# 128-row products around attention, and operand loads in two column parts, in a one-core window-attention block

## The reference

```python
hp = jnp.pad(layer_norm(x, ln1_g, ln1_b), ...)      # 16 x 16 -> 28 x 28, windows of 14 x 14
q, k, v = split_heads(windows(hp) @ qkv_w + qkv_b)  # 12 heads of 16
attn = (q * scale) @ k.T + bias_h(q, rel_h) + bias_w(q, rel_w)
o = softmax(attn) @ v
x2 = x + unwindow(o @ proj_w + proj_b)[:, :16, :16]
h2 = layer_norm(x2, ln2_g, ln2_b)
out = x2 + gelu(h2 @ mlp_w1 + mlp_b1, approximate=False) @ mlp_w2 + mlp_b2
```

## Time and profile before

| | |
|---|---|
| time of the runs | 338.98 us median of 3 (336.39 to 343.41) |
| the profiled execution | 338.49 us, span 336.6 us |
| busy | PE 294.4 us (87%), DVE 165.6 (49%), ACT 129.2 (38%), POOL 84.4 (25%) |
| one product of L933 | over 128 rows 654 ns, over 64 rows 642 ns (mean, 24 each) |
| granted TensorE clock | 0.912 on average |
| chain that ended last | PE 60%, DMA 21% (of it `qop<-bias` 16%), SP's queue 8%, DVE 6% |

### The profile page before, as it was taken

The page is one execution under the profiler, slowest core; times in us unless marked ns, Lnnn a source line. Parts: engine busy times, 40 slices in busy tenths (PEclk is TensorE's granted clock), DMA queues, the critical chain, the costliest instruction groups (busy, mean ns, idle before and its releaser), DMA issues.

```text
span 336.6 us, 5235 instructions
## 1 busy us (share of the span) xinstructions
PE 294.4 (87%) x1980; PEld 201.8 (60%) x1980; DVE 165.6 (49%) x435; ACT 129.2 (38%) x245; POOL 84.4 (25%) x131
## 2 busy tenths in 40 slices
PE   0799979999889778878888878699898999999996
PEld 0433376557466556656566556448766657868696
DVE  4953384126567567646675677246489211111011
ACT  1144654223546456535553555453001444140400
POOL 3294631003001133303341433470046600000000
PEclk9999998999959999979997999858755699999999
DMA  6660042994005679765864585830000000101011
GB/s 185 172 159 0 2 81 50 177 179 83 1 2 100 121 127 167 126 127 99 173 139 103 105 170 147 214 90 13 14 0 1 0 2 0 47 2 47 0 49 47
DMA packets 19409, 27.94 MB, mean 83 GB/s; under 512 B 6052, under 2 KB 16196, under 8 KB 17560
## 3 DMA queue, kind: packets, MB, share of 16 engines
q1 hardware_dynamic: 16840, 24.95, 34.9%
q0 software_dynamic: 2016, 2.46, 3.8%
q10 hardware_dynamic: 528, 0.20, 0.4%
HBM read 5.81 MB, written 1.57 MB: 22 GB/s over the span
## 4 chain that ended last, share of the span: by engine, by line
PE 60%; DMA 21%; SPq 8%; DVE 6%; issue 2%; ACT 1%; ACTq 0%; DVEq 0%
DMA qop<-bias 16%; PE ps L1229 12%; PE ps L1244 9%; PE ps L933 7%; PE ps L988 6%; PE ps L968 5%; PE ps L1193 3%; PE ps L1022 3%; PE ps L1087 2%; PE ps L1061 2%; SPq L300 2%; DMA qop<-shift_rest 2%; SPq L301 2%; PE ps L917 2%; PE ps L1134 2%
## 5 line engine op out<-in xcount | busy, mean ns | idle before, releaser
L756 DVE TENSOR_REDUCE nmax<-ps 98x2 f32<-98x392 f32 x96 | 53.4, 566 | 41.3 <-PE ps L1022 39.9
L1022 PE MATMUL ps<-kop,qop 126*98 126x196 f32 x192 | 39.2, 291 | 10.8 <-DMA qop<-bias 8.3
L565 ACT ACTIVATE pm<-ps 98x784 f32<-98x784 f32 x48 | 39.4, 830 | 18.5 <-PE ps L1061 18.4
L1022 PEld LDWEIGHTS ps<-kop,qop 126*98 126x98 f32 x192 | 25.7, 176 | 22.3 <-DMA qop<-bias 12.3
L1244 PE MATMUL ps<-w2t,gl 128*128 128x192 f32 x192 | 32.0, 328 | 0.0
L1061 PE MATMUL ps<-qop,kop 128*98 128x196 f32 x192 | 29.0, 278 | 3.3 <-DMA qop<-shift 2.5
L1244 PEld LDWEIGHTS ps<-w2t,gl 128*128 128x128 f32 x192 | 31.1, 190 | 0.7 <-issue 0.7
L761 DVE TENSOR_REDUCE nmax<-ps 120x1 f32<-120x316 f32 x48 | 23.1, 485 | 15.9 <-PE ps L1028 14.6
L633 ACT ACTIVATE gl<-ps,b 128x512 f32<-128x512 f32 x24 | 16.4, 688 | 35.2 <-PE ps L1229 35.1
L437 POOL DMA_DIRECT2D den<-osb x11 | 7.1, 645 | 80.8 <-ACT osb L582 80.8
L1061 PEld LDWEIGHTS ps<-qop,kop 128*98 128x98 f32 x192 | 23.9, 186 | 5.2 <-DMA qop<-shift 2.6
(11 more groups left out here) (129 smaller groups left out, 457.9 us busy)
## 6 DMA issues: line engine op xcount, KB each, us to landing
qop<-bias SPq DMA_DIRECT2D x8, 448.0 KB
kop<-hl SPq DMA_DIRECT2D x12, 280.5 KB
qop<-hl SPq DMA_DIRECT2D x12, 256.0 KB
kop<-hl SPq DMA_DIRECT2D x12, 140.2 KB
bias<-in_x SPq DMA_DIRECT2D x4, 384.0 KB, 4.6
qop<-hl SPq DMA_DIRECT2D x12, 128.0 KB
xres<-in_x SPq DMA_DIRECT2D x2, 768.0 KB, 7.4
out<-xn SPq DMA_DIRECT2D x8, 192.0 KB, 2.0
```

What stands on the lines that cost most here:

```text
L565: a.activation(pm[0:HALF, gi], ps[0:HALF, b0:b0 + 2, 0:2 * WIN], ACT.Exp).then_inc(s["exp_done"], 1)
L756: v_.tensor_reduce(nmax[0:HALF, h % 2, 2 * n:2 * n + 2], ps[0:HALF, bank, 0:2 * WIN].rearrange("p (t k) -> p t k", t=2), AX.X, ALU.max, ne ...
L1022: o = mm(ps[0:HALF, bank, WIN * t:WIN * (t + 1)], q[0:R_MAX, WIN * n + HALF * t:WIN * n + HALF * (t + 1)], kk[0:R_MAX, WIN * n:WIN * (n + ...
```

## The change

It has two parts, which are independent in the code.

**Operand loads in two column parts.** `load_operands(h, part)` loads the columns 0 to 1568 of `qop` and `kop` (part 0) or the rest of both (part 1), with the same DMAs on fewer columns. Part 0 waits for `st_done` of 6 (h - 3) + 4, the last reader of the main columns (`weights(h-3, 3)`), part 1 for all six. `load_low_biases` does the same on POOL. The rest parts have semaphores of their own, for which `score_piece(h, 8)` waits.

**Products over 128 rows.** The tiles `ht1`, `wq1`, `wqp[1]`, `on1`, `wp1` and `w11l` have 128 rows. POOL clears rows 64 to 127 of `ht1`, `wq1`, `wp1` and `on1` by four memsets; the products that read these tiles run over 128 rows. The last product of `hidden` takes `w11l` and `h2s` over all 128 rows, so a product of two low parts is added to the result. `on1` moves from the address of `split` to that of `pm`.

```diff
@@ load_operands @@
-            def load_operands(h):
+            def load_operands(h, part):
                 (tq, rq), (tk, rk) = place(h)
-                q, k, sl = qop[h % RING].bitcast(F32), kop[h % RING].bitcast(F32), op_in[h % RING]
+                c0, c1, c2 = ((0, MAIN, MAIN), (MAIN, T, KCOLS))[part]
+                q, k, sl = qop[h % RING].bitcast(F32), kop[h % RING].bitcast(F32), (op_in, rest_in)[part][h % RING]
                 if h >= RING:
-                    sp.wait_ge(s["st_done"], 6 * (h - RING + 1))
+                    sp.wait_ge(s["st_done"], 6 * (h - RING) + (4, 6)[part])
...
-                src = hl[tq][rq:P:A8, :, 0:T]
-                sp.dma_start(q[0:2 * KD], src).then_inc(sl, 16)
-                sp.dma_start(q[2 * KD:R_BIAS], src[:, 0]).then_inc(sl, 16)
+                src = hl[tq][rq:P:A8, :, c0:c1]
+                sp.dma_start(q[0:2 * KD, c0:c1], src).then_inc(sl, 16)
+                sp.dma_start(q[2 * KD:R_BIAS, c0:c1], src[:, 0]).then_inc(sl, 16)
...
                 if h and h + 2 < HEADS:
-                    load_operands(h + 2)
+                    for part in range(2):
+                        load_operands(h + 2, part)
@@ POOL @@
+            for n, a_ in enumerate((ht1, wq1)):
+                g.memset(a_[C - P:P], 0.0).then_inc(s["ht_zero"], 1)
+                pool.wait_ge(s["ht_zero"], n + 1)
             pool.wait_ge(s["w_in"], 2 * 16)
...
-                pool.wait_ge(s["st_done"], 6 * (h - RING + 1))
                 pool.wait_ge(s["blo_ready"], 16)
...
+                for part, (c0, c1) in enumerate(((0, MAIN), (MAIN, T))):
+                    pool.wait_ge(s["st_done"], 6 * (h - RING) + (4, 6)[part])
...
             pool.wait_ge(s["late_in"], N_LATE)
+            g.memset(wp1[C - P:P], 0.0).then_inc(s["wp_zero"], 1)
+            pool.wait_ge(s["wp_zero"], 1)
...
             store_heads_output(HEADS - 2)
-
+            pool.wait_ge(s["xpb_ready"], NCH)
+            pool.wait_ge(s["pv_done"], 4 * HEADS - 2)
+            g.memset(on1[C - P:P], 0.0).then_inc(s["wp_zero"], 1)
+            pool.wait_ge(s["wp_zero"], 2)
@@ TensorE @@
+                if n == B:
+                    pe.wait_ge(rest_in[h % RING], operands_loaded(h))
+                    if h >= A8:
+                        pe.wait_ge(low_rest_in[h % RING], low_biases_loaded(h))
...
                     if u == 0:
                         pe.wait_ge(s["b1_ready"], 1)
+                        pe.wait_ge(s["wp_zero"], 2)
...
-                             (w11s, h2s[:, c % 2]), (w11l, h2s[0:C - P, c % 2]))
+                             (w11s, h2s[:, c % 2]), (w11l, h2s[:, c % 2]))
```

More of the change, by code:

```diff
@@ L139, in window_attention_block @@
         xt = bias8[:, 0].rearrange("p l t -> p (l t)")[:, 0:NT * C].rearrange("p (t c) -> p t c", t=NT)
-        wqp = [bias8[:, 0].rearrange("p l t -> p (l t)")[0:r, NT * C + 3 * P * k:NT * C + 3 * P * (k + 1)]
-               for k, r in enumerate((P, C - P))]
+        wqp = [bias8[:, 0].rearrange("p l t -> p (l t)")[:, NT * C + 3 * P * k:NT * C + 3 * P * (k + 1)]
+               for k in range(2)]
         htw = (bias4[:, 0], bias4[:, 1])
-        _, (qop2, kop2, ppad, osb, prest, ot0, pm) = room(
+        pm_at, (qop2, kop2, ppad, osb, prest, ot0) = room(
             split, ("qop2", [ROWS, T], F32R), ("kop2", [ROWS, KCOLS], F32R), ("ppad", [P, 2, B * REST]),
-            ("osb", [P, 2, QUAD]), ("prest", [PAIR, B * REST]), ("ot0", [P, T]), ("pm", [P, 4, 2, 2 * WIN]))
-        _, (on1,) = room(split, ("on1", [C - P, T]))
+            ("osb", [P, 2, QUAD]), ("prest", [PAIR, B * REST]), ("ot0", [P, T]))
+        _, (pm,) = room(pm_at, ("pm", [P, 4, 2, 2 * WIN]))
+        _, (on1,) = room(pm_at, ("on1", [P, T]))
         rd = nc.alloc_sbuf_tensor_at("rd", [2 * A8, 2, T], F32R, offset=gl_at)
@@ L264, in _ @@
             load_x(1)
-            for wt, r0, r1 in ((wq0, 0, P), (wq1, P, C)):
+            for wt, r0, r1 in ((wq0, 0, P), (wq1[0:C - P], P, C)):
                 sp.dma_start(wt[:], qkv_w[r0:r1]).then_inc(s["w_in"], 16)
@@ L320, in _ @@
             sp.dma_start(wpe1[:], proj_w[P:C]).then_inc(s["wpe_in"], 16)
-            load_operands(0)
-            load_operands(1)
+            for h in range(2):
+                for part in range(2):
+                    load_operands(h, part)
             sp.wait_ge(s["bias_done"], 8)
@@ L326, in _ @@
             lay_constants(2)
-            load_operands(2)
+            for part in range(2):
+                load_operands(2, part)
             sp.wait_ge(s["vshift_ready"], 1)
@@ L441, in load_low_biases @@
                 n = HEADS - A8
-                pool.wait_ge(s["st_done"], 6 * (h - RING + 1))
                 pool.wait_ge(s["blo_ready"], 16)
[L444 to L447, removed]
+                for part, (c0, c1) in enumerate(((0, MAIN), (MAIN, T))):
+                    pool.wait_ge(s["st_done"], 6 * (h - RING) + (4, 6)[part])
+                    for a_ in range(2):
+                        r0 = 64 * a_ + h - A8
+                        pool.dma_start(qop[h % RING].bitcast(F32)[R_BIAS + 2 * a_ + 1:R_MASK:4, c0:c1],
+                                       bias4[r0:r0 + n * (WS - 1) + 1:n, 1, c0:c1]
+                                       ).then_inc((low_in, low_rest_in)[part][h % RING], 16)
             for h in range(HEADS - 2):
```

48 lines of the change are left out of this document (28 added, 20 removed).

## The result

| | before | after |
|---|---|---|
| time of the runs beside each other | 340.34 us median | 313.49 us median of 4 (311.29 to 316.44) |
| ratio | | 0.926, 95% interval 0.914 to 0.939 |
| the profiled execution | 338.49 us, span 336.6 | 313.16 us, span 311.3 |
| granted clock on average | 0.912 | 0.923 |

The account below looks back on a forecast made before the run. The prediction took attention's loop through load_operands to bound the kernel. 338.5 - 6.3 (operand load in two parts) - 3.4 (products over 128 rows, through the clock) = 328.8 us, range 320 to 341 us.

Parts of the forecast that it names:

- What bounds the kernel: Attention: a loop through load_operands, repeated nine times in 99.8 us, with 12.3 us of waits for its loads.
- Operand load in two parts: Attention: the operand-load wait goes, the wait for qop<-shift takes its place; nine heads take 93.5 us against 99.8, -6.3 us.
- The small load thus takes about its turn by arrival: Attention: qop<-shift moves behind two of SP's loads, landing 4.3 us after issue, or 5.4 us in four cycles.
- I count nothing: End of attention: late loads come earlier and the 2.5 us wait may move to the head before; no gain counted.
- SP's issues: Operand loads: ten issues of 0.6 us, 6 us in a 10 us cycle, hidden since SP's queue stands idle otherwise.
- Products over 128 rows: First stage, values, projection, hidden: 64 more rows add no busy time, only the clock can move; -3.4 us.
- The clock: In hidden: at a higher granted clock ten products take 2.88 us, not 5.50, the next thirty 9.04, not 9.86; -3.4 us.
- 9.0 us assumed for a cycle: Attention: one head's cycle with no wait for any DMA, from 8.76 us of TensorE busy plus some 0.3 us.
- Memsets: POOL's clears of the added rows, 2.3 us early and 1.8 us over on1, are hidden.
- Rival 1: Attention: the small load doesn't wait its turn, nine heads take 81.0 us, -18.8 us, total 316.3 us; chance 0.12.
- Rivals 2 and 4: Attention: 2, new wait eats the gain, 335.1 to 340.3 us, chance 0.24; 4, slower, 350.3 us, chance 0.10.
- rival 3: Hidden: the clock isn't lifted, so only the attention gain remains, total 332.2 us; chance 0.12.

Follow-up runs that it names:

- f1_changed: The changed kernel itself, word for word, run again on one chip beside three variants: 312.62 us median.
- f2_wait5: Changed kernel, but the main part of an operand load waits for five parts of weights, not four: 307.83 us, ratio to before 0.907.
- e6_hidden64: Changed kernel with only the last product of each result in hidden over 64 rows again: 323.55 us.
- e1_rows64: Changed kernel with all its 128-row products over 64 rows again, so the load split alone is left: 327.27 us, ratio to before 0.970.
- e3_pairs64: As e1_rows64, but every second result takes its terms in reverse, so there are half as many row-count changes: 318.71 us.
- e4_proj64: Changed kernel with only the projection over 64 rows again: 312.09 us, ratio to before 0.927.
- f4_no_loads: Changed kernel with operand and low bias loads left out from head 3 on, so its results are not the block's: 302.06 us, ratio to before 0.887.
- f3_cut_late: Changed kernel with loads still cut in two, but both parts waiting for all six parts of weights: 308.65 us, ratio to before 0.906.

## Why the prediction was right or wrong

**What bounds the kernel.** Right for attention: the loop through `load_operands` was the bound, its wait for `qop<-bias` fell from 12.3 us to nothing in the loop, and with one load it came back whole (16.3 us, of it 2.4 at head 0). The chain ends on this load eight times, not nine: one cycle (169.28 to 180.73 us) ends on `qop<-shift_rest`. It was not asked what bounds the first stage and `hidden`, where TensorE stands in the chain: each product's distance to the next.

**Operand load in two parts: -6.3 us.** -7.5 us in the first trace of after, -5.3 in the second (116.8 us), -6.2 in the split alone. Over the nine heads of the forecast, 93.5 us were expected and 91.7 (after) and 93.8 (`f1_changed`) measured, 99.8 before. The term was right in size; its working was right in half. The mechanism held that `qop<-shift` becomes what the cycle ends on. "The small load thus takes about its turn by arrival" did not hold as a rule: with the 4.3 us that it gave for L (the time from the issue of `qop<-shift` to its landing), no cycle could be under 9.9 us, and four were 9.2 to 9.4. Its packets and SP's from 120.5 to 122.5 us, then its packets to 123.4:

```profile
q1 hardware_dynamic: 112, 0.41, 87.5%
...
q10 hardware_dynamic: 16, 0.01, 1.2%
```
```profile
q10 hardware_dynamic: 18, 0.01, 4.2%
```

It moved amid SP's packets; L was 3.73 us. For the heads from 5 on L was 4.2 to 5.7 us, and 10.4 to 11.6 us cycles lie about the forecast's 11.0. The two errors nearly cancelled. "I count nothing" for the late loads was wrong too: the wait at the last head lasted 6.34 us from the issue. Nor was there a need to start early; the last section of experiments shows that the cut alone gives as much or more. SP's issues were taken at 6 us a head; with two bias loads in each part they take 9.3 us (145.91 to 150.68 and 150.72 to 155.24 us in `f2_wait5`), a whole cycle. That was hidden still.

**Products over 128 rows: -3.4 us.** This is the step that failed: "L933 takes as long over 64 rows as over 128 (the table above): no busy time is added", and with it that only the clock can move. The two means are alike (654 and 642 ns) because in both groups every second matmul of L933 stands right behind one of the other row count, so that both carry the price of the change. In after the mean of the same line is 597 ns. The first stage measured -8.8 us (4.2 of it in `project` by the chain, 6.57 + 6.13 + 12.47 against 5.28 + 5.15 + 10.53 us; eighty matmuls of `values` at 0.51 us for eight are up to 5.1) and `hidden` -7.6 (76.75 us in `e6_hidden64` against 69.13), where nothing was counted but the clock. A group of before that I had not split by operands has it in plain sight; L1229, with counts, busy us and mean ns:

```profile
L1229 PE MATMUL ps<-h2h,w10h 128*128 128x512 f32 x24 | 12.8, 534 | 0.8 <-issue 0.8
L1229 PE MATMUL ps<-h2s,w11l 64*128 64x512 f32 x24 | 12.5, 519 | 0.0
L1229 PE MATMUL ps<-h2l,w10h 128*128 128x512 f32 x24 | 10.2, 425 | 0.0
L1229 PE MATMUL ps<-h2h,w10l 128*128 128x512 f32 x24 | 10.2, 424 | 0.0
L1229 PE MATMUL ps<-h2s,w11s 128*128 128x512 f32 x24 | 10.1, 419 | 0.0
```

The product over 64 rows and the one right behind it take 100 ns longer than the three that have neighbours of their own kind.

**The clock.** It was at 1.00 when `hidden` began in after (0.50 from 223.3 to 240.37 us, `hidden` from 242.21), as forecast. That filled rows in the projection raise it in time was my estimate, from the earlier trace rows: 0.50 beside the 64-row products of 242.1 to 258.6 us, 1.00 beside the 128-row ones of 229.9 to 235.0 us. The traces bear it out as far as they go. With the projection over 64 rows the clock rose 20.0 to 25.3 us after its first product, 3.5 to 8.9 us into `hidden` (four traces: before, `e1_rows64`, `e3_pairs64`, `e4_proj64`); with it over 128 rows 10.6 to 16.0 us after it, before `hidden` (nine traces, in three of which it fell again inside `hidden`). The tenth, `f4_no_loads`, is an exception: there it was low again until 3.7 us into `hidden`. Only `e4_proj64` differs from after in this alone, in one trace. But no run shows the term of 3.4 us; what the runs show in its place is less: before minus `e6_hidden64` leaves 78.1 - 76.75 = 1.3 us at most, and `e1_rows64` and `e6_hidden64` are alike (76.9 and 76.75), as are `e4_proj64` and after. The rest became the wait for ScalarE's first Gelu.

**Rivals.** Rival 1 (small load not held up, 316.3 us) came nearest by its time, for another reason: attention gave 7.5 us and not 18.8. In part it was right, in heads 1 to 4: of the packets counted above, `qop<-shift` moved 16 from 120.5 to 122.5 us while SP's queue moved 112, so it did not wait for SP's to end, nor was it turn by turn. Rivals 2 and 4 fell, and so did rival 3: the clock was up before `hidden`, though that brought almost nothing. The 9.0 us assumed for a cycle with no wait for a DMA was measured as 9.12 to 9.16 (`f4_no_loads`, heads 1 to 7). **Memsets**: nothing seen of them on the path, as said.

## What to carry to other kernels

Look at how far apart the starts of neighbouring products are, split by operand and shape, before you say that a shape costs nothing: a mean over products that all stand beside the other shape hides the price of alternating (654 and 642 ns here, 597 ns once the shapes were alike). Where results are sums over a full and a half contraction, it is worth a try to fill the half with zeros (here 0.13 to 0.17 us for each change between 64 and 128 rows), or, if there is no room, to reverse every second result so that like row counts meet (8.6 us in `e3_pairs64`). Before you start a transfer earlier, ask which small, urgent transfer it will then be in front of; here it was enough to cut off what isn't needed first (308.65 us in `f3_cut_late`, 312.62 with the earlier start).

## What the hardware showed that I had not expected

A weight load ran under the running product where both had 128 rows (no idle time before it, products 0.23 us apart, 287.22 to 288.38 us in after), also at 126 and 128 (64.34 us in before), and where both had 64:

```profile
290.79 0.29 PEld L1257 LDWEIGHTS ps<-h2s,w11l 64*128 64x128 f32 x2 [0.36 <-issue]
```

In this line of `e3_pairs64` the 0.36 us stand before the first load, behind a product over 128 rows; the second follows with no idle time, and the products over 64 rows of both take 0.73 us together. Where the row count changed between 64 and 126 or 128, the load started only near the end of the product before it (311.18 us against 311.26 in before): 0.16 us a change in `project`, 0.17 us in `hidden`, 0.13 us in `values`. What in the chip makes the difference is not shown by any run.
